# A fused two-layer graph network on one core: normalisation sums taken from accumulators, squares on ScalarE, node sums from transposed copies, new step tables

## The reference, cut to what matters

```python
# layer 0 on x (8, 2048, 128), adj (8, 2048, 2048); C = 32 blocks of k = 64
Wh = h @ W;  e = leaky(Wh @ a, 0.2)
out = softmax(adj_block * e) @ Wh_block
y = leaky(out @ W1 + b1, 0.01); y = leaky(y @ W2 + b2, 0.01); y = y @ W3 + b3
z = layernorm(y + out) * ln_g + ln_b
x1 = _layernorm(x + z)
# layer 1, H = 4 heads, dh = 32
h = (x1 @ W_proj.T).reshape(B, N, H, dh)
scores = leaky_relu(s_left[:, :, None, :] + s_right[:, None, :, :] + adj[..., None] * we, 0.2)
scores = scores - 9e15 * (adj <= 1e-5)
agg = softmax(scores, axis=2) @ h
out = leaky_relu(x1 + agg + bias, 0.5)
result = _layernorm(x1 + out)          # (x - mean) / sqrt(var + 1e-5)
```

## Time and profile before

| | before |
|---|---|
| median of 3 runs | 2027.68 us |
| profiled execution, its time | 2030.75 us |
| its span, first to last instruction | 2028.7 us |
| granted TensorE clock, mean | 0.972 |
| GpSimd busy | 1858.8 us, 92% |
| VectorE busy | 1855.1 us, 91% |
| TensorE busy | 1833.7 us, 90% |
| ScalarE busy | 1563.7 us, 77% |
| DMA moved | 191.69 MB, 94 GB/s |

### The profile page before, as it was taken

How to read it: one execution, slowest core, us unless ns; L and a number is a source line. 1 busy time by engine, 2 the same in 40 slices (tenths; PEclk the granted TensorE clock), 3 DMA queues, 4 the chain that set the end, 5 groups by cost and what they waited for, 6 DMA issues and landing times.

```text
span 2028.7 us, 34544 instructions
## 1 busy us (share of the span) xinstructions
PE 1833.7 (90%) x11304; PEld 913.2 (45%) x11304; DVE 1855.1 (91%) x3529; ACT 1563.7 (77%) x3448; POOL 1858.8 (92%) x664
## 2 busy tenths in 40 slices
PE   5779999999999999999999999999989999888885
PEld 4644444445444544444444444445445444433332
DVE  1259998999989999999999999899998999999997
ACT  6657887888878878779877888788877887766664
POOL 2069999999999999999999999999999999999996
PEclk7779999999999999999999999999999999999999
DMA  3122333333233342424323323332322333243220
GB/s 98 64 70 83 105 109 100 97 97 110 88 106 97 95 114 68 121 94 115 99 82 123 94 88 105 97 118 84 110 83 97 118 89 97 73 123 99 92 65 11
DMA packets 138618, 191.69 MB, mean 94 GB/s; under 512 B 22344, under 2 KB 56520, under 8 KB 138440
## 3 DMA queue, kind: packets, MB, share of 16 engines
q1 hardware_dynamic: 138440, 189.49, 31.4%
HBM read 180.82 MB, written 8.65 MB: 93 GB/s over the span
## 4 chain that ended last, share of the span: by engine, by line
DVE 41%; PE 23%; issue 19%; POOL 13%; ACT 3%; SPq 1%; DVEq 0%; DMA 0%; ACTq 0%; POOLq 0%
DVE X L1012 28%; PE psum L1108 19%; POOL X L471 12%; DVE X L1002 5%; PE psum L1265 4%; DVE x1s L900 1%; DVE st L873 1%; POOL haug L456 1%; DVE est L873 1%; DVE res L960 1%; DVE lky L966 1%; DVE psum L951 1%; ACT o_sb L628 1%; DVE mv L879 0%; PE psum L1184 0%
## 5 line engine op out<-in xcount | busy, mean ns | idle before, releaser
L471 POOL TENSOR_TENSOR X<-RHO,E 128x1536 f32<-128x1536 f32 (+1 forms) x512 | 1776.2, 3502 | 75.5 <-ACT E L727 71.4
L1012 DVE SCALAR_TENSOR_TENSOR X<-psum,s_j,X 128x512 f32<-128x512 f32 x2048 | 1399.2, 741 | 51.3 <-POOL X L471 46.3
L1108 PE MATMUL psum<-X,haug 128*33 128x512 f32 x4096 | 991.9, 605 | 3.1 <-DVE X L1012 3.1
L727 ACT ACTIVATE E<-psum,we_s 128x512 f32<-128x512 f32 x512 | 397.1, 776 | 254.3 <-PE psum L1108 253.0
L1265 PEld LDWEIGHTS psum<-ident,adj_sb 128*128 128x128 f32 x2048 | 288.4, 141 | 577.7 <-DVE X L1012 412.4
L1265 PE MATMUL psum<-ident,adj_sb 128*128 128x128 f32 x2048 | 434.9, 293 | 112.0 <-DVE X L1012 105.6
L1108 PEld LDWEIGHTS psum<-X,haug 128*33 128x33 f32 x4096 | 196.1, 111 | 428.8 <-issue 392.4
L732 ACT ACTIVATE psum<-psum,we_s 128x512 f32<-128x512 f32 x512 | 381.2, 745 | 0.0
L1108 PE MATMUL psum<-sgn_ident,pen 128*128 128x128 bf16 x2048 | 378.4, 220 | 0.0
L690 ACT ACTIVATE pen<-adj_sb,pen_bias 128x512 bf16<-128x512 f32 x512 | 367.0, 717 | 0.4
L1002 DVE TENSOR_TENSOR X<-psum,E 128x512 f32<-128x512 f32 x496 | 334.7, 675 | 2.9 <-ACT psum L534 2.9
(11 more groups left out here) (220 smaller groups left out, 1511.1 us busy)
## 6 DMA issues: line engine op xcount, KB each, us to landing
adj_sb<-in_adj_dram SPq DMA_DIRECT2D x128, 1024.0 KB, 5.1
RHO<-rho_scratch SPq DMA_DIRECT2D x32, 1024.0 KB, 9.8
out_dram<-o_sb SPq DMA_DIRECT2D x32, 256.0 KB, 2.9
xg<-in_x_dram SPq DMA_DIRECT2D x28, 256.0 KB, 5.6
blk<-in_adj_dram SPq DMA_DIRECT2D x56, 64.0 KB, 5.3
X<-in_x_dram SPq DMA_DIRECT2D x2, 256.0 KB, 3.2
W_sb<-in_L_gnn_W_dram SPq DMA_DIRECT2D x4, 64.0 KB, 2.1
X<-in_adj_dram SPq DMA_DIRECT2D x4, 64.0 KB, 3.4
```

Source lines behind the costliest of these rows:

```text
L471: Q.tensor_tensor(X[m % NX][:, 0:heads, :], RHO[:, g % 2, 0:heads, :], bc(E[m % NE][:], 1, [P, heads, GROUP]), ALU.mult).then_inc(B_pool, 1)
L727: A.activation(E[m % NE][:], TA[m % NT], ACT.Exp, scale=we_s[:, 3:4], bias=we_s[:, 5:6]).then_inc(E_sb, 1)
L1012: ins = V.scalar_tensor_tensor(slot[:, h, :], TA[m % NT], s[:, k, h:h + 1], slot[:, h, :], ALU.mult, ALU.max)
L1108: return T.matmul(o, l, r, start=start, stop=stop)
```

## The change

Statistics of the two outer normalisations: bn_stats and bn_aggr go from VectorE. The sum of each row comes from the accumulator output of the instruction that makes the row; ScalarE squares the deviation from the mean, with an accumulator, and takes Ln and Exp of the sum. lky becomes four instructions instead of one, each with an accumulator. The x1T copy on ScalarE gets an accumulator output, and hsum multiplies the projection weights by these sums: 4 matmuls instead of 16; TINY moves into hcol's scale. haug's four pieces get places of their own, 58, 59, 62 and 65 (place 1 of the next body). Most tables are given anew, and the two four-head tiles move from 7 and 35 to 11 and 29.

```diff
-    FOUR = (7, 35)
+    FOUR = (11, 29)
-    AT_PE = {"xT": (-26, -19, 0, 18), "wh0": (-25, -17, 0, 18), "wh1": (-24, -16, 5, 19), "ST": (-11, 7, 20, 29),
-          "oT": (-10, 10, 21, 32), "y1": (-9, 11, 22, 33), "y2": (-8, 12, 23, 34), "z0": (-7, 13, 24, 35),
-          "z1": (-7, 14, 25, 36), "g0": (-4, 16, 27, 37), "g1": (-2, 17, 28, 39), "x1T": (6, 26, 41, 48),
-          "h0": (7, 27, 43, 49), "h1": (9, 29, 44, 50)}
-    AT_ACT = {"xT": (-23, -16, 2, 20), "wh0": (-22, -15, 7, 21), "wh1": (-21, -13, 8, 21),
-          "logits": (-21, -13, 9, 23), "exp": (-19, -8, 12, 26), "soft": (-15, -7, 19, 30), "ST": (-8, 12, 23, 33),
-          "oT": (-7, 13, 24, 35), "y1": (-6, 14, 25, 36), "y2": (-5, 15, 26, 36), "ssq": (-2, 17, 28, 39),
-          "z_rstd": (-2, 19, 28, 40), "r_rstd": (4, 22, 35, 44), "r_norm": (6, 25, 38, 48), "x1T": (8, 29, 45, 50),
-          "h0": (10, 30, 46, 52), "h1": (12, 32, 49, 52)}
-    AT_DVE = {"max": (-20, -9, 10, 25), "rin": (-16, -8, 13, 27), "res": (0, 19, 30, 41), "r_stats": (2, 20, 33, 42)}
-    AT_POOL = {"xb": (-24, -8, 20, 27), "r_shift": (5, 23, 37, 45)}
-    ONCE_PE = {"rmT": 52, "Rb": 53, "rhoT": 56, "hsum": 58}
-    ONCE_ACT = {"diag": 55, "factors": 58, "rho": 59, "hcol": 63}
+    AT_PE = {"xT": (-26, -20, 0, 18), "wh0": (-26, -17, 0, 18), "wh1": (-24, -16, 5, 19), "ST": (-11, 7, 20, 29),
+          "oT": (-10, 10, 21, 32), "y1": (-9, 11, 22, 33), "y2": (-8, 12, 24, 34), "z0": (-7, 13, 25, 35),
+          "z1": (-6, 14, 25, 36), "g0": (-3, 16, 27, 37), "g1": (-3, 17, 27, 40), "x1T": (5, 25, 42, 48),
+          "h0": (8, 27, 44, 49), "h1": (9, 28, 45, 50)}
+    AT_ACT = {"xT": (-24, -16, 2, 20), "wh0": (-23, -15, 6, 21), "wh1": (-21, -13, 9, 22),
+          "logits": (-21, -13, 9, 25), "exp": (-19, -10, 13, 27), "soft": (-15, -5, 19, 30), "ST": (-8, 12, 23, 32),
+          "oT": (-7, 13, 24, 34), "y1": (-6, 14, 25, 35), "y2": (-5, 14, 27, 36), "ssq": (-2, 17, 28, 39),
+          "z_rstd": (0, 19, 28, 39), "r_rstd": (3, 22, 37, 44), "r_norm": (6, 24, 40, 49), "x1T": (7, 29, 46, 50),
+          "h0": (10, 29, 46, 52), "h1": (13, 31, 48, 52)}
+    AT_DVE = {"max": (-20, -13, 12, 26), "rin": (-18, -6, 16, 27), "res": (1, 19, 30, 42)}
+    AT_POOL = {"xb": (-24, -8, 20, 25), "r_shift": (5, 24, 39, 45), "haug": (58, 59, 62, 65)}
+    ONCE_PE = {"rmT": 52, "Rb": 53, "rhoT": 55, "hsum": 56}
+    ONCE_ACT = {"diag": 55, "factors": 57, "rho": 58, "hcol": 61}
     ONCE_DVE = {"rm": 52, "R4": 54, "lam": 55}
-    ONCE_POOL = {"haug": 59}
-    ONCE_SP = {"rho": 54}
-    EPI_PE = {"back0": 1, "back1": 3}
+    ONCE_SP = {"rho": 49}
+    EPI_PE = {"back0": 2, "back1": 3}
     EPI_ACT = {"acc": 2, "prelu": 7, "rstd": 10, "norm": 15}
-    EPI_DVE = {"part0": 3, "part1": 5, "stats": 7}
-    EPI_POOL = {"shift": 12}
+    EPI_DVE = {"part0": 4, "part1": 5, "lky": 6}
+    EPI_POOL = {"shift": 15}
...
-            def invstd(log, out, minus, mean_var):
-                A.activation(log, mean_var[:, :, 1], ACT.Ln, bias=eps_c[:])
-                link(copy(minus, mean_var[:, :, 0], -1.0))
+            def invstd(log, out, minus, sums, sq, src):
+                link(copy(minus, sums, -1.0 / D))
+                for t in range(GT):
+                    ins = A.activation(squares[:, t, :], src(t), ACT.Square, bias=minus[:, t:t + 1],
+                                       accum_out=sq[:, t:t + 1])
+                link(ins)
+                link(A.activation(log, sq, ACT.Ln, scale=1.0 / D, bias=eps_c[:]))
                 return A.activation(out, log, ACT.Exp, scale=-0.5)
...
-                copy(x1T_of(c), tail_bank(c)).then_inc(x1T_sb, 1)
+                if c % NB == 0 and c > 0:
+                    act.wait_ge(hsum_ps, c // NB)
+                A.activation(x1T_of(c), tail_bank(c), ACT.Copy,
+                             accum_out=x1sum[:, c % NB:c % NB + 1]).then_inc(x1T_sb, 1)
...
                 for t in range(GT):
                     ins = V.scalar_tensor_tensor(x1_of(c)[:, t, :], mid_bank(c)[:, tsl(t)], rstd[s][:, t:t + 1],
-                                                 xb[s][:, t, :], ALU.mult, ALU.add)
+                                                 xb[s][:, t, :], ALU.mult, ALU.add,
+                                                 accum_out=rsum[s][:, t:t + 1])
...
-                V.tensor_tensor(lky[:], BK_B.rearrange("p (t f) -> p t f", t=GT), x1_of(g)[:], ALU.add).then_inc(lky_sb, 1)
+                for t in range(GT):
+                    ins = V.scalar_tensor_tensor(lky[:, t, :], BK_B[:, tsl(t)], 1.0, x1_of(g)[:, t, :], ALU.mult, ALU.add,
+                                                 accum_out=esum[:, t:t + 1])
+                ins.then_inc(lky_sb, 1)
...
-            def make_hsum(nb, j):
+            def make_hsum(nb):
                 pe.wait_ge(rho_sb, nb + 1)
-                for t in range(CHUNK * j, CHUNK * (j + 1)):
-                    ins = mm(BK_A[:, 0:1], hb[:, t, 0:D], tiny[:], start=(t == 0), stop=(t == JT - 1))
-                if j == NC_ - 1:
-                    ins.then_inc(hsum_ps, 1)
+                pe.wait_ge(x1T_sb, NB * (nb + 1))
+                for u in U:
+                    ins = mm(BK_A[:, 0:1], WpT[:, 0:D], x1sum[:, u:u + 1], start=(u == 0), stop=(u == NB - 1))
+                ins.then_inc(hsum_ps, 1)
```

More of the change, by code:

```diff
@@ L713, in epi_rstd @@
             def epi_rstd(g):
[L714 to L715 removed]
+                act.wait_ge(lky_sb, g + 1)
+                invstd(elog[:], erstd[:], enmu[:], esum[:], esq[:], lambda t: lky[:, t, :]).then_inc(erstd_sb, 1)
             def epi_norm(g):
@@ L869, in _ @@
             V = nc.vector
-            def moments(st, src, done):
-                for t in range(GT):
-                    ins = V.bn_stats(st[:, t, :], src(t))
-                ins.then_inc(done, 1)
-            def mean_var(st, out, ready, count, done):
-                dve.wait_ge(ready, count)
-                for t in range(GT):
-                    V.bn_aggr(out[:, t, :], st[:, t, :]).then_inc(done, 1)
             def chain_max(c):
@@ L986, in epilogue @@
                         (epi_rden, epi_scale, epi_add)[part](g - 1, r)
-                if k == EPI_DVE["stats"]:
-                    (epi_lky, epi_moments, epi_var)[part](g - 1)
+                if k == EPI_DVE["lky"] and part == 0:
+                    epi_lky(g - 1)
             def tile(m):
@@ L1033, in host @@
                             residual(c)
-                        if n == AT_DVE["r_stats"][u] and part < 2:
-                            (r_moments, r_var)[part](c)
                     if n == ONCE_DVE["rm"] and part == 0:
@@ L1383, in _ @@
                 transposes(m)
-            for j in range(NC_):
-                make_hsum(0, j)
+            make_hsum(0)
             for m in range(-BODY // 2, 0):
```

63 lines of the change are left out of this document (17 added, 46 removed).

## The result

The changed kernel takes 2018.13 us (median of six, 2015.49 to 2020.93); the kernel before, on the same chip, 2027.05 (six, 2023.67 to 2028.10). The ratio is 0.996, 95% interval 0.9947 to 0.9973: 8.9 us less, 0.4%. The sign was right and the time lies in the range, which took in no change and a slower kernel too. The size was not right: 23.1 us were forecast, more than twice what came.

A forecast was written before the change was run, and what follows sets the result against it. The prediction took GpSimd's busy time as each body's floor, with 52.1 us of main-loop idle above it winnable. Loop -24.9, ahead +0.7 and behind +1.1 gave -23.1 us: 2004.6 us, range 1987 to 2036.

The forecast's parts named there:

- Stalls after, per body: GpSimd's idle time in a full body: 7.0 us becomes 3.3, so -3.7; bounds 1.4 and 6.9.
- Added: New GpSimd stalls per body: 1.0 us in places 22 to 29, 0.5 from 37 to 53, none at 58.
- convoy: Stall at a fixed place where engines wait on each other: 1.98 us at 57, 1.38 at 37, 0.95 at 22, 0.86 at 0.
- the floor: GpSimd's busy time, 231.68 of a 238.7 us body, as least body length; only idle above it can be won.
- a ring over three tiles: Loop through TensorE, E, GpSimd and VectorE: up to 9.4 us against three tiles of 10.4; slack 1 to 2.5 us.
- The third rival: The change doesn't do what it says: reads cost VectorE 0.19 each, removed stalls return elsewhere; 2027.7 us, chance 0.08.
- VectorE: Busy time -4.2 us a body (bounds -6.8 and -0.7), reads at 0.08 each; no direct gain, since GpSimd is the floor.
- ScalarE: Each invstd block 2.26 us instead of 0.53, eight a body, +13.8 (bounds +12 and +18); busy about 208.5 a body.
- ScalarE late: Rival: blocks fall where VectorE lags; slower once over 38% of 13.8 us a body reaches GpSimd; 2051 us at 60%, chance 0.16.
- E's wait for TensorE: Sign of ScalarE late: E's idle wait for TensorE vanishes while GpSimd's wait for E grows.
- The new wait: VectorE's lky, moved to place 6, waits for Prelu in ScalarE's 7: 0.5 us, bounds 0 and 1.
- Ahead and behind: Outside the loop: ahead +0.7 us (blocks +6.3, hsum -5.2, z_rstd -0.45), behind +1.1.

The follow-up runs named there:

- one_square: The changed kernel with one of the four Squares in each ScalarE block, leaving out work the result needs: 1996.19 us, ratio 0.9852.
- two_moves: The changed kernel with two ScalarE steps moved, first group's x1T from place 7 to 8 and its soft from 49 to 53: 2012.62 us, ratio 0.9934.
- before_four1: The kernel before with one four-head tile a body (place 7) instead of two, 35 being shared again: 2023.84 us, ratio 0.9990.
- the single moves: Two kernels, each the kernel before: lky and its statistics at place 6 (2028.81 us); ScalarE's pairs y1, y2 and wh0, wh1 pulled apart (2025.20 us).
- before_one_stat: The kernel before with bn_stats on one of four parts of each group, leaving out statistics the result needs: 2010.53 us, ratio 0.9927.
- squares_twice: The changed kernel with the four Squares of each block made twice: 2132.61 us, ratio 1.0524.

## Why the prediction was right in its sign and wrong in its size

**The step that failed** is "Stalls after, per body". It took 5.2 us off the 7.0 by cause, let 1.8 stay, added 1.5 and got 3.3. The causes did vanish: at 57, 0 and 22 nothing stands, at 37 0.12, and nearly all of the other 1.8 went too. But 5.1 us of new stalls stand in their place, and the term that was mis-sized is "Added". From 23 to 29 it has 0.8 us (1.0 forecast), from 35 to 51 3.3 (0.5 forecast), and at 8 0.75 (nothing forecast). With 0.3 more of GpSimd's busy time a body falls by 1.6 and not by 3.7, and that, body by body, is the whole miss of 14 us (-24.9 forecast for the loop, -10.9 measured). one_square and two_moves show what made them: three of four squares in each block hold 1.8 us of the 5.1, and the two places 7 and 49 hold 1.7, of which 0.65 comes back at 11 when they are cleared. The place 7 is a convoy of the kind that the prediction had just found, made anew: x1T moved from 8 to 7 and waits 1.78 us there. Only what is left, at 35 to 37 above all, was not traced to a cause by a run.

Under it lies the sentence that GpSimd's busy time is the floor and the idle above it can be taken off item by item. before_four1 refutes it for the full bodies: 1.1 us less of the one was 1.3 more of the other. The four engines form a ring over three tiles (VectorE's end of m, TensorE's transposes of m+3, E, GpSimd, VectorE), which the prediction itself had summed to 9.4 of 10.4 us, and whose slack it then spent on every place anew. In the kernel before, relief of VectorE came through in part (1.8 of 4.0 us a body) and relief of GpSimd not at all; that VectorE was the longer part of the ring is what this and the chain (41% against 13%) suggest, and no run shows it for each place. TensorE, 23% of that chain, was not relieved alone in any run. The third rival had a mechanism of this kind ("each stall taken away returns in the next tight place"), at 0.08; the single moves gained as little as it says, and it was wrong on VectorE's relief.

That the sign came out is in part luck. The sum rested on convoys taken away, and the two attempts to take them out of the kernel before gained nothing; what helped beside it was VectorE's relief, which the prediction had put at no direct gain.

**VectorE.** Forecast -4.2 a body, measured -6.0, near the lower bound of -6.8. The term was mis-sized in the accumulator reads and in lky. Timeline of VectorE, lky in the changed kernel (its answer to the earlier trace rows):

```profile
672.66 0.29 DVE L951 SCALAR_TENSOR_TENSOR lky<-psum,x1s 128x128 f32<-128x128 f32 x1 [1.09 <-ACT psum L714]
672.88 0.08 DVE L951 DVE_READ_ACCUMULATOR lky<-psum,x1s 128x1 f32 x1
672.88 0.28 DVE L951 SCALAR_TENSOR_TENSOR lky<-psum,x1s 128x128 f32<-128x128 f32 x1
...
673.51 0.69 DVE L978 TENSOR_TENSOR X<-psum,E 128x512 f32<-128x512 f32 x1
```

The read begins when the next instruction does, and costs it next to nothing: four instructions take 673.51 less 672.66, 0.85 us, against the 1.05+0.32 forecast. Of the residual, four with reads take 1.08 us (median from the first start to the next row), where four without took 1.03, 0.01 for each read. The two-instruction rule of the Trainium skill ("VectorE: DVE Perf Modes", section "Two Vector instructions with no wait between them") is what the trace shows: the read has a row of its own. Its price here is near zero. That VectorE's relief is "no direct gain" was the wrong conclusion: before_one_stat, which relieves it by 4.0 us a body and changes nothing else, is 0.7% faster than the kernel before, 13 us of the 15 in the loop.

**ScalarE.** Forecast 208.5 a body, measured 207.4; a block forecast at 2.26, measured 2.37:

```profile
723.88 0.21 ACT L529 ACTIVATE nmu<-rsum 128x4 f32<-128x4 f32 x1
724.12 0.40 ACT L607 ACTIVATE squares<-x1s,nmu 128x128 f32<-128x128 f32 x1
724.43 0.19 ACT L607 ACTIVATION_READ_ACCUMULATOR squares<-x1s,nmu 128x1 f32 x1
724.52 0.39 ACT L607 ACTIVATE squares<-x1s,nmu 128x128 f32<-128x128 f32 x1
...
726.25 0.71 ACT L693 ACTIVATE pen<-adj_sb,pen_bias 128x512 bf16<-128x512 f32 x1
```

A square steps on after 0.40 and 0.39, as taken. This block stands at 37, and 0.84 us at 38 is its stall. Its cost to the body was put at 1.0 for 22 to 29 and 0.5 after; one_square shows 0.69 at 23 and 28 and 1.45 at 38 and 45, less 0.55 that appears at 41 instead. So the second half was mis-sized. The 1.07 at 50 was seen as a place of 5.1 us and priced into the same 0.5; it stands with one square as with four, and went with a move. Of the 5.1 us of stalls after, 3.3 forecast, 1.8 go with three of the four squares and 3.3 do not.

**ScalarE late** (the rival on the other side): its condition was that more than 38% of the added time reaches GpSimd. one_square shows a quarter (2.1 of 8.2). squares_twice shows it for the next 13 us, with the clock as said above.

**E's wait for TensorE** did shrink, the first half of what should show this rival. The groups after of E, of L467, and of the penalty, whose adjacency load is queued behind the rho store:

```profile
L467 POOL TENSOR_TENSOR X<-RHO,E 128x1536 f32<-128x1536 f32 (+1 forms) x512 | 1778.5, 3505 | 53.5 <-ACT E L730 49.5
...
L730 ACT ACTIVATE E<-psum,we_s 128x512 f32<-128x512 f32 x512 | 395.2, 772 | 139.6 <-PE psum L1076 137.7
...
L693 ACT ACTIVATE pen<-adj_sb,pen_bias 128x512 bf16<-128x512 f32 x512 | 366.7, 717 | 1.0
```

E's idle time was 254.3 us in the kernel before. In body 2 E now starts with under 0.1 us of idle in 48 of 64 tiles (39 before), and VectorE follows GpSimd within 0.15 us in 30 (16 before). The second half, a longer wait of GpSimd, did not come: 75.5 is 53.5. The penalty waits 1.0 us in all, so the later load harms nobody, as was forecast.

**TensorE, and what moved past queues.** hsum at 56 left no stall at 58. The ST step of 53 waits no more for lky (2.90 in the earlier trace rows); what it still waits is for ScalarE's diagonal:

```profile
792.04 0.38 PE L1076 MATMUL psum<-diagR,ones 4*128 4x4 f32 x2 [0.51 <-ACT diagR L529]
792.36 0.63 PE L1152 MATMUL psum<-ident,blk 128*64 128x128 f32 x4
```

**The new wait.** VectorE's wait for Prelu was put at 0.5 us, bounds 0 and 1, four times a body; the sum has it only in its upper bound and at nothing in the middle. It is 12.2 us over the kernel, about 1.5 a body, and in body 2 it comes twice: 1.09 at place 23 (above) and 0.57 at 39. No stall of GpSimd stands three tiles behind either.

**Ahead and behind.** The first haug starts between 86.90 and 88.67 in the four profiles with the old prologue, mean 87.7, and at 93.69 in the changed kernel, +6.0 for 6.3 forecast. hsum and the first step behind it:

```profile
97.16 1.00 PE L1076 MATMUL psum<-x1sum,WpT 128*128 128x1 f32 x8
98.03 0.60 PE L1152 MATMUL psum<-ident,blk 128*64 128x128 f32 x4
```

That is 0.87 us for 6.80 in the profiled before, but 3.94 in before_four1, so -3.1 to -5.9 for the -5.2 forecast: the 6.93 of the earlier trace rows was read at a clock of 0.50. In all about +1.0 for +0.7, inside the scatter. The tail gave +0.2 for +1.1: lky and its sums take 0.97 us up to ScalarE's next, not 1.4, and 0.4 came off ahead of lky, which the sum did not have.

**Left open.** Which place a removed stall moves to was seen, not derived; a tile-by-tile count of the ring, with VectorE's lag carried over, would be needed. Neither single move in the kernel before was a clean removal, so what one gives there is open. The moves of the new table were not tried one by one on the changed kernel, beyond two_moves.
